# Causal attention beside routed experts in one kernel: the mask moved to TensorE, all low halves to GpSimd, the shift row laid by a DMA

## What is computed

```python
xn = layernorm(x)
# branch 1: causal attention, 16 heads of 64
q, k, v = split(rmsnorm(xn) * gamma @ w_qkv)          # per head 1024 x 64
sim  = (q * 64 ** -0.5) @ k.T
sim  = where(key later than query, -max, sim)
attn = softmax(sim) @ v
# branch 2: each token goes through the 2 best of 8 experts (128 -> 512 -> 128), then a layer norm
out = x + attn @ w_out + experts(xn)
```

## Time and profile before

| | |
|---|---|
| median of 3 runs | 1635.53 us (1633.17 to 1636.81) |
| span of the profiled execution | 1691.3 us |
| its own time | not given apart from the span |
| TensorE matmul busy | 1453.6 us (86%), 8490 instructions |
| TensorE weight load busy | 1161.8 us (69%) |
| VectorE busy | 1351.2 us (80%) |
| ScalarE busy | 1124.1 us (66%) |
| GpSimd busy | 951.0 us (56%) |
| mean granted TensorE clock | 0.945 of full speed |

### The profile page before, as it was taken

The page is one execution under the profiler, slowest core; times in us unless marked ns, Lnnn a source line. Parts: engine busy times, 40 slices in busy tenths (PEclk is TensorE's granted clock), DMA queues, the critical chain, the costliest instruction groups (busy, mean ns, idle before and its releaser), DMA issues.

```text
span 1691.3 us, 36531 instructions
## 1 busy us (share of the span) xinstructions
PE 1453.6 (86%) x8490; PEld 1161.8 (69%) x8491; DVE 1351.2 (80%) x3877; ACT 1124.1 (66%) x2590; POOL 951.0 (56%) x1690
## 2 busy tenths in 40 slices
PE   3253999959999899999989998999999989999998
PEld 3242888837777767776777676767777777777766
DVE  6351555548999799889988998899899979998995
ACT  2141666638678777776777777777777777778675
POOL 0724000028667766676668565856686668567765
PEclk9756999979999999999999999999999999999998
DMA  8101111112012111111111111111111111111111
GB/s 288 51 28 45 56 56 56 47 35 51 20 31 48 45 23 33 37 46 26 31 30 45 26 31 30 45 26 31 29 45 31 27 29 45 31 26 39 34 29 47
DMA packets 57837, 73.02 MB, mean 43 GB/s; under 512 B 6888, under 2 KB 43536, under 8 KB 57616
## 3 DMA queue, kind: packets, MB, share of 16 engines
q1 hardware_dynamic: 39696, 52.31, 13.1%
q10 hardware_dynamic: 13824, 9.86, 1.8%
q0 software_dynamic: 4096, 8.40, 1.6%
HBM read 20.47 MB, written 16.52 MB: 22 GB/s over the span
## 4 chain that ended last, share of the span: by engine, by line
PE 37%; DVE 21%; issue 15%; POOL 4%; ACT 2%; DVEq 1%; DMA 0%; POOLq 0%; SPq 0%; ACTq 0%
PE max_ps L1346 5%; DVE unread L1170 5%; PE score_ps L1370 5%; PE score_ps L1371 4%; PE misc_ps L1405 4%; PE head_ps L1388 4%; PE head_ps L1392 4%; PE head_ps L1390 4%; DVE p_lo L1288 3%; PE misc_ps L1331 2%; DVE k_b L1154 2%; PE misc_ps L1353 2%; DVE q_a L1154 2%; POOL p_lo L1061 2%; DVE shift L1179 2%
## 5 line engine op out<-in xcount | busy, mean ns | idle before, releaser
L1061 POOL TENSOR_TENSOR p_lo<-probs,p_hi 128x512 fp32r<-128x512 f32 (+2 forms) x512 | 502.7, 985 | 185.5 <-ACT p_hi L1111 162.0
L1111 ACT ACTIVATE probs<-score_ps 128x512 f32<-128x512 f32 (+3 forms) x768 | 375.2, 489 | 221.8 <-PE score_ps L1371 208.0
L1111 ACT ACTIVATE p_hi<-score_ps 128x512 fp32r<-128x512 f32 (+3 forms) x768 | 373.8, 487 | 0.0
L1170 DVE CUSTOM_DVE_ANT_0 unread<-max_ps,mask 128x512 bf16<-128x512 f32 (+3 forms) x512 | 299.3, 585 | 62.5 <-PE max_ps L1346 57.7
L1053 POOL TENSOR_SCALAR_AFFINE_SELECT probs<-probs 128x128 f32<-128x128 f32 x512 | 188.9, 369 | 253.7 <-ACT p_hi L1111 251.0
L1346 PE MATMUL max_ps<-k_a,q_a 128*128 128x512 f32 (+3 forms) x768 | 282.6, 369 | 48.0 <-DVE row_max L1170 36.6
L1388 PE MATMUL head_ps<-p_hi,v_hi 128*65 128x512 f32 (+3 forms) x768 | 294.9, 384 | 1.7 <-DVE p_lo L1288 1.4
L1370 PE MATMUL score_ps<-q_a,k_a 128*128 128x512 f32 (+3 forms) x768 | 271.6, 354 | 18.7 <-issue 17.8
L1371 PE MATMUL score_ps<-q_b,k_b 66*128 66x512 f32 (+3 forms) x768 | 272.9, 355 | 0.0
L1392 PE MATMUL head_ps<-p_lo,v_hi 128*65 128x512 f32 (+3 forms) x768 | 263.1, 343 | 0.0
L1390 PE MATMUL head_ps<-p_hi,v_lo 128*64 128x512 f32 (+3 forms) x768 | 263.0, 342 | 0.0
(11 more groups left out here) (172 smaller groups left out, 2474.5 us busy)
## 6 DMA issues: line engine op xcount, KB each, us to landing
k_a<-k_a SPq DMA_DIRECT2D x64, 256.0 KB
q_b<-q_a SPq DMA_DIRECT2D x64, 256.0 KB
sorted_x<-zeros SPq DMA_DIRECT2D x13, 384.0 KB, 16.1
w_raw<-sorted_x SPq DMA_DIRECT2D x26, 192.0 KB, 2.5
sorted_y<-result ACTq DMA_DIRECT2D x78, 64.0 KB, 1.6
acc<-in_L_attn_x_dram SPq DMA_DIRECT2D x4, 512.0 KB, 8.5
w_raw<-in_L_ffn_W_dram ACTq DMA_DIRECT2D x1, 2048.0 KB, 23.3
x_row<-in_L_attn_x_dram SPq DMA_DIRECT2D x8, 256.0 KB
```

Source lines behind the costliest of these rows:

```text
L1061: pool.tensor_tensor(p_lo[:, slot, 0:w], probs[:, slot, 0:w], p_hi[:, slot, 0:w].bitcast(F32), ALU.subtract).then_inc(pool_split, 1)
L1111: ins = act.activation(p[:, (g * CH + c) % RING, 0:width], score_ps[(g * CH + c) % 2][:, 0:width], ACT.Exp, scale=SCALE)
L1170: dve.tensor_tensor_reduce(out=unread[:, m % 2, 0:width], in0=max_ps[:, m % 2, 0:width], in1=mask[:, end - width:end], scale=1.0, scalar=s ...
```

## The change

- The mask of a diagonal chunk is a third matmul into the score bank: a bfloat16 identity times a triangle of -1e30 (`later`), 128x128. GpSimd's two selects go.
- All 12 low halves of a group are GpSimd's; VectorE has none. `probs` is a ring of 4, and ScalarE waits, before it writes a chunk's `probs`, until the low half four chunks back is made (`p_split`).
- The shift is one row instead of two. VectorE makes no halves. TensorE turns the four columns of `row_max` of a half head in one transpose, ScalarE rounds the 4x128 result with a scale of -1 into `shift`, and SyncE lays it by a DMA (4 pieces of 128) as the 65th row of `q_b`. The turning stands one chunk earlier: at c7 and at c1.
- The scores at c0 and c4 wait for that DMA, with one semaphore per half; the bank of `misc_ps` is free when ScalarE has read it.

The diff, cut to its core:

```diff
+            PROBS = 4
+            probs = sb(ph2, "probs", [P, PROBS, BANK])
+            shift = sb(ph2, "shift", [GROUP, 2, P], F32R)
-                if g + 1 < final and c == 8:
+                if g + 1 < final and c == 7:
                     order.append(("shift", g + 1, 0))
-                if g < final and c == 2:
+                if g < final and c == 1:
                     order.append(("shift", g, 1))
...
+                    def lay_shift(hp, g, half):
+                        sp.wait_ge(shift_turned, n_half(hp, g, half) + 1)
+                        row = q_b[g // 2 % 2][g % 2][HEAD:HEAD + 1, half * BANK:(half + 1) * BANK]
+                        sp.dma_start(row.bitcast(F32).rearrange("o (t p) -> o t p", p=P),
+                                     shift[:, half].bitcast(F32)).then_inc(shift_done[half], 16)
...
-                            if DIAG[c]:
...
-                            if not BY_DVE[c]:
...
+                            w = WIDTH[c]
+                            pool.tensor_tensor(p_lo[:, slot, 0:w], probs[:, (g * CH + c) % PROBS, 0:w],
+                                               p_hi[:, slot, 0:w].bitcast(F32),
+                                               ALU.subtract).then_inc(p_split, 1)
...
-                        act.activation(dst[HEAD:HEAD + 2, half * BANK:(half + 1) * BANK], misc_ps[u % 2][0:2, :],
-                                       ACT.Copy).then_inc(shift_done, 1)
+                        act.activation(shift[:, half], misc_ps[u % 2][0:GROUP, 0:P], ACT.Copy,
+                                       scale=-1.0).then_inc(shift_turned, 1)
...
+                                if hp_first or (g * CH + c) >= PROBS:
+                                    act.wait_ge(p_split, n_chunk(hp, g, c) - PROBS + 1)
...
-                    def max_hi(hp, g, half):
...
-                    def max_lo(hp, g, half):
...
-                        pe.wait_ge(max_split, n_half(hp, g, half) + 1)
-                        for q in range(GROUP):
-                            ins = pe.transpose(dst[0:2, q * P:(q + 1) * P],
-                                               shift[:, g % 2, half * GROUP + q, :].bitcast(F32), ident[:])
-                        ins.then_inc(misc_ready, 1)
+                        pe.wait_ge(max_taken, n_max(hp, g, HALF_MAX[half]) + 1)
+                        pe.transpose(dst[0:GROUP, 0:P], row_max[:, g % 2, half * GROUP:(half + 1) * GROUP],
+                                     ident[:]).then_inc(misc_ready, 1)
...
-                            pe.wait_ge(shift_done, n_half(hp, g, half) + 1)
+                            pe.wait_ge(shift_done[half], hp * (16 * G) + (16 * g + 16))
                         pe.matmul(dst, k_a[i][s][:, keys], q_a[i][s][:, qs], start=True, stop=False)
-                        pe.matmul(dst, k_b[i][s][:, keys], q_b[i][s][:, qs], start=False,
-                                  stop=True).then_inc(scores_ready, 1)
+                        ins = pe.matmul(dst, k_b[i][s][:, keys], q_b[i][s][:, qs], start=False, stop=not DIAG[c])
+                        if DIAG[c]:
+                            ins = pe.matmul(dst[:, 0:P], ident16[:], later[:], start=False, stop=True)
+                        ins.then_inc(scores_ready, 1)
```

More of the change, by code:

```diff
@@ L750, in attention_and_experts @@
         v_done = sem("v_done")
-        pool_split = sem("pool_split")
-        dve_split = sem("dve_split")
+        p_split = sem("p_split")
         copies_done = sem("copies_done")
-        shift_done = sem("shift_done")
+        shift_turned = sem("shift_turned")
+        shift_done = [sem(f"shift_done{i}") for i in range(2)]
         scores_ready = sem("scores_ready")
         probs_ready = sem("probs_ready")
-        diag_masked = sem("diag_masked")
         pv_done = sem("pv_done")
@@ L791, in attention_and_experts @@
             mask = sb(ph2, "mask", [P, SEQ])
+            ident16 = sb(ph2, "ident16", [P, P], BF16)
+            later = sb(ph2, "later", [P, P], BF16)
             unread = sb(ph2, "unread", [P, 2, BANK], BF16)
             row_max = sb(ph2, "row_max", [P, 2, TILES])
-            shift = sb(ph2, "shift", [P, 2, TILES, 2], F32R)
+            shift = sb(ph2, "shift", [GROUP, 2, P], F32R)
             rden = sb(ph2, "rden", [P, 2, 4])
@@ L818, in attention_and_experts @@
             WIDTH = [(half + 1) * BANK - q0 for half, _, q0 in chunks]
-            BY_DVE = [DIAG[c] and WIDTH[c] > 2 * P for c in range(CH)]
             LAG = 4
-            SPLIT_LAG = 2
+            CONSTS = 8
             G = BATCH * 2
@@ L1029, in _ @@
                             pool.wait_ge(attn_consts, n)
-                            pool.memset(k_b[i][s][HEAD:HEAD + 2, :].bitcast(F32), 1.0).then_inc(attn_consts, 1)
+                            pool.memset(k_b[i][s][HEAD:HEAD + 1, :].bitcast(F32), 1.0).then_inc(attn_consts, 1)
                             n += 1
                     pool.wait_ge(attn_consts, n)
+                    pool.tensor_copy(ident16[:], ident[:]).then_inc(attn_consts, 1)
+                    pool.affine_select(out=later[:], in_=later[:], pattern=[[1, P]], compare_op=ALU.is_ge,
+                                       fill=MASKED, base=0, channel_multiplier=-1).then_inc(attn_consts, 1)
+                    pool.wait_ge(attn_consts, CONSTS)
                     def walk(hp, order, last):
@@ L1283, in walk @@
                                 combine(hp, g)
-                            elif kind == "low" and BY_DVE[c]:
-                                half, j, q0 = chunks[c]
-                                slot, width = (g * CH + c) % RING, (half + 1) * BANK - q0
-                                dve.wait_ge(diag_masked, n_diag(hp, g, c) + 1)
-                                dve.tensor_tensor(p_lo[:, slot, 0:width], probs[:, slot, 0:width],
-                                                  p_hi[:, slot, 0:width].bitcast(F32),
-                                                  ALU.subtract).then_inc(dve_split, 1)
                     run(walk, dve)
```

72 lines of the change are left out of this document (14 added, 58 removed).

## The result

The changed kernel took **1577.11 us** (median of 4 runs, 1574.81 to 1583.17), the kernel before, on the same chip, 1636.17 us. The ratio is 0.965, 95% interval 0.963 to 0.968. That is 59 us less (57 against the 1634.3 us that the kernel before took beside the later runs), where 23 were forecast: the sign was right, but the forecast gain was less than half of the measured one. The time lies in the range, near none of the rivals' times.

The account below looks back on a forecast made before the run. TensorE was taken as the bound, waiting for VectorE. Terms -75 - 7 - 34 + 56 + 22 + 9 = -29 us, less 5 held back, gave -24 on 1691.3, scaled to 1612 us; range 1560 to 1668 us.

Parts of the forecast that it names:

- What bounds the kernel: Attention: TensorE is the bound and VectorE the engine it waits for, which holds it back by 75 us.
- All terms but the mask: VectorE waits -75, half clock behind `combine` -7, transposes -34, bank wait +22, shift's DMA +9, VectorE's remaining bursts +5 us.
- -75: Attention: TensorE's waits for VectorE, for row maxima and the shift's halves, go with VectorE's removed work: -75 us.
- The transposes: TensorE's turning of the shift: 384 of 512 transposes go, at 0.09 us each: -34 us.
- The step that failed: Diagonal chunks' scores on TensorE: 512 added mask matmuls of 128 columns at 0.11 us each: +56 us.
- The bank of the turning: Transpose at c1 (even groups) and c7 (odd) waits for VectorE to read the projection's bank: 14 + 8 = +22 us.
- The shift's DMA: Scores at c4 and c0 wait for the shift's row; landing taken as 2.0 us: +9 us, between nothing and 61.
- The row lands late: Rival, scores at c4 of odd groups and c0 behind the copies: 3.1 us landing, +28 us, 1663 us; chance 0.12.
- The mask is dear: Rival, mask matmuls: without overlap 0.28 us each, +63 us, 1696 us; break-even 0.16 us; chance 0.07.
- GpSimd is late: Rival, group 1, c7 to c11: gathers between low halves delay GpSimd, +8 us, 1643 us; chance 0.08.
- ScalarE takes VectorE's place: Rival, even groups: ScalarE's projections hold TensorE, only odd groups gain, -39 instead of -75, 1647 us; chance 0.07.
- Marks: Signs if right: VectorE near 1035 us busy, row-maxima waits under 15, mask 0.11, transposes x128, shift's DMA waits under 20 us.

## Why the prediction was right and wrong

- **What bounds the kernel**: right. TensorE is the bound and VectorE what it waits for; of the 52.6 us that went in the attention, 44.3 were idle time of TensorE.
- **All terms but the mask**: -75 - 7 - 34 + 22 + 9 + 5 = -80 us; the kernel without the mask, measured, is 86 us under the one before. As a sum right within 6 us, which is in part luck, since inside it errors cancel. The transposes gave 41 us (a turning stands 0.02 to 0.03 us in the row where four took 0.35), not 34; the waits for row maxima fell to 13.6 us, not 5; the clock is 0.97 in the attention and was 0.96. One term is missing: the forecast took all of TensorE's time beside the two listed waits for its own work, but 16.1 us of it were the wait for `wqk_lo`, and 9.9 of them went, as VectorE's step there fell from 1357 to 414 ns.
- **The step that failed**: "The mask has a 128-column load ahead and one behind it, so I take 0.11: **+56 us**." The price in the row was right (0.113, 58 us). Wrong was to enter it whole in the sum of time. TensorE stands idle for other engines, and what it does more shortens that: 96.3 us idle in the attention without the mask, 73.2 with it. The term measured +29 us. With -6 from the others that is the gap: -24 - 6 - 27 = -57 us.
- The same error runs through "-75": it is the sum of the waits, and their worth depends on what else fills them. In the kernel before, 58 us of masks cost 9 us.
- **The bank of the turning**, +22: the printed wait is 24.8 us in 30 instead of 14 at c1, and taking it away gave 14.4 us. For time the 14 was right, but by luck: I had worked out 0.45 us for each, and in the timeline shown one is 2.25 us long, behind `combine`, with half clock after it, while 10 of the 24.8 us printed were worth no time. At c7 no wait of a size to be listed came.
- **The shift's DMA**, +9: waits of 3.6 us in all. The landing was 1.73 us alone (2.0 taken), 3.83 behind the copies. The Trainium skill, DMA: Bandwidth & Descriptors, section "Anatomy of one DMA", fits about 2.0 us of fixed cost for a DMA on GpSimd's path; for this 2 KB transfer between tiles of SBUF on SyncE's queue, 1.60 to 1.73 us were measured where it stands alone in the chains.
- **The row lands late**: refuted here (3.6 us of waits), and by little: one more landing of 1.6 us costs 89 us.
- **The mask is dear**: refuted; 0.113 in the row, under the 0.16 of its break-even.
- **GpSimd is late**: refuted here (0.3 us of waits). It comes true in the kernel with the new shift and all low halves that keeps the selects (39.3 us), and there at the place that the rival names, beside the gathers (27 us of it). In `combine` the last steps, the product with `fgamma` and the sum into `acc`, which read two tiles of SBUF, took 1321 and 1544 ns instead of 683 and 693. The timelines of the changed kernel show a step of GpSimd under way when the product starts:

```profile
1065.22 1.29 POOL L1039 TENSOR_TENSOR p_lo<-probs,p_hi 128x512 fp32r<-128x512 f32 x1 [0.69 <-ACT p_hi L1091]
```

```profile
1065.74 1.32 DVE L1196 TENSOR_TENSOR x_row<-x_row,fgamma 128x512 f32<-128x512 f32 x1
```

VectorE's step ends 0.55 us after GpSimd's. In the kernel with shift and low halves, where GpSimd has all low halves too, the same two steps took 682 and 692 ns: there no low half of GpSimd was under way when they started. So it is the meeting that counts, not how much GpSimd has; `wqk_lo` is the reverse case: it met a step of GpSimd before the change and meets none after it. The Trainium skill, SBUF — State Buffer, section "SBUF: two separate sides", calls the shared port pair an exclusive lock for the whole instruction; the trace agrees. The forecast read from it that moving work to GpSimd costs: the low halves' move cost 8 us beside the mask with the old shift and gained 29 with the new one.

- **ScalarE takes VectorE's place**: refuted; TensorE's only listed wait for ScalarE is 0.8 us, once, and it was there before.
- Marks: VectorE's 1035 us busy was wrong, it is 1126.3. The removed groups are 315.8 us by printed durations, but most of VectorE's instructions begin before the printed end of the one before, and `combine` got longer; busy time in the attention fell by 225. Row maxima under 15 us: right (13.6). Mask 0.11: right (0.113). Transposes x128, row waits under 20 us: right.
- The profiled execution's extra 57 us lay outside the attention. Scaling the sum by it moved it by under 1 us.

## What to carry to other kernels

Work added to the bound engine costs less than its place in the row when other engines hold that engine from time to time. Here the share was 9 of 58 us in the kernel before, 29 of 58 in the changed one: measure it by leaving the piece out or by doubling it, rather than by the row alone. Before a step is given to another engine, count what that engine has in the same chunk; two moves can each lose (16 and 27 us here) and together win (14), when one makes the room for the other. When the totals of all engines have room, the places of the long steps are worth as much as the steps: 21 us lost and 19 won with the same instructions.

## What was not expected of the hardware

- A bfloat16 matmul of 128 columns between fp32 ones starts the next after 0.04 us, but that next one, with a full load of 128 columns behind the mask, takes 0.08 to 0.09 us longer from its start to the following start. A second mask with the same weights adds 0.05.
- Printed durations of VectorE sum to 1113 us in the attention of the changed kernel and its busy time is 966 us: two of three of its instructions begin before the printed end of the one before (1067.32 for 0.74 us, the next at 1067.99).
- The granted clock was near half behind the wait of 2.25 us (0.57 over 3.75 us) and behind the pair of 0.88 and 0.76 us (0.50 over 3.00 us), and full behind one of the turning's common waits of 0.4 us (timeline and window of the changed kernel below). The 3 us at half clock behind the pair cost 1.5 us, about as much as the two waits themselves.

```profile
1033.20 0.27 PE L1306 MATMUL misc_ps<-ident,row_max 128*4 128x128 f32 x1 [0.40 <-DVE q_a L1134]
```

```profile
1033.20:1037.20 4.00, 4.00 (x22) 2.99 (x23) 3.74 (x10) 3.16 (x8) 1.90 (x3) 1.00 0.00 1
```
